# Attention's work lists made cyclic over the batch's end, and PSUM shared as two banks for value sums and two in the ring

## What is computed

```python
x = layernorm(x + attention(x))     # 16 heads of 16 channels, causal
x = layernorm(x + experts(x))       # 8 experts, each token goes to 2; only the first 1024 rows
```

```python
outs.append(_sdpa(q[:, :6], k[:, :6], v[:, :6], 1 / sqrt(16)))          # 6 dot-product heads
outs.append(_hyp_attn(q[:, 6:10], k[:, 6:10], v[:, 6:10], curvature))   # 4 hyperbolic heads
outs.append(_sdpa(qn, kn, v[:, 10:], sqrt(16)))                         # 6 heads of unit q and k
# in _hyp_attn: arg = max(-curv * (q.k - tq * tk), 1 + 1e-7)
#               scores = 1 / (1e-6 + sqrt(1/curv) * arccosh(arg)) + causal mask
```

## Time and profile before

| | us |
|---|---|
| median of 3 runs | 2300.5 (2297.19 to 2304.39) |
| the profiled execution | 2313.54, span on the core 2312.0 |
| TensorE busy | 1806.9 (78%) |
| VectorE busy | 1422.5 (62%) |
| ScalarE busy | 1422.3 (62%) |
| GpSimd busy | 683.8 (30%) |

### The profile page before, as it was taken

The page is one execution under the profiler, slowest core; times in us unless marked ns, Lnnn a source line. Parts: engine busy times, 40 slices in busy tenths (PEclk is TensorE's granted clock), DMA queues, the critical chain, the costliest instruction groups (busy, mean ns, idle before and its releaser), DMA issues. The chain is left out here.

```text
span 2312.0 us, 39981 instructions
## 1 busy us (share of the span) xinstructions
PE 1806.9 (78%) x13330; PEld 965.2 (42%) x13330; DVE 1422.5 (62%) x3280; ACT 1422.3 (62%) x1400; POOL 683.8 (30%) x332
## 2 busy tenths in 40 slices
PE   6888888843887896897797787888789689746994
PEld 3434443421333443343344343444434334325893
DVE  4767676772663776676676777776777667650113
ACT  1333333321887888788788888788788878811110
POOL 0000000001443534444444444543444365510002
PEclk9999999975997998998998999999899899878997
DMA  5222333328026006207306304504502620119972
GB/s 190 85 103 109 110 110 110 110 107 166 1 45 96 11 16 125 66 1 122 83 2 113 92 2 84 121 2 70 126 11 31 137 55 23 42 51 350 345 276 66
DMA packets 88461, 217.50 MB, mean 94 GB/s; under 512 B 14112, under 2 KB 34848, under 8 KB 83936
## 3 DMA queue, kind: packets, MB, share of 16 engines
q1 hardware_dynamic: 79840, 184.74, 30.5%
q0 software_dynamic: 8448, 30.41, 4.2%
HBM read 146.52 MB, written 68.58 MB: 93 GB/s over the span
## 5 line engine op out<-in xcount | busy, mean ns | idle before, releaser
L1067 ACT ACTIVATE a_PT<-a_s 128x1024 f32<-128x1024 f32 (+3 forms) x576 | 461.3, 808 | 206.8 <-PE a_s L889 135.0
L886 PE MATMUL a_s<-a_Q,a_K 96*128 96x512 bf16 (+7 forms) x1152 | 331.3, 350 | 157.0 <-ACT a_PT L1067 108.7
L1245 DVE TENSOR_REDUCE a_mx<-a_w 128x1 f32<-128x512 f32 (+2 forms) x576 | 305.9, 550 | 53.0 <-PE a_w L917 36.8
L1145 POOL TENSOR_TENSOR a_Z<-a_Z,a_R 128x2182 f32<-128x2182 f32 x64 | 290.4, 4537 | 94.0 <-ACT a_R L1079 94.0
L1142 POOL TENSOR_TENSOR a_R<-a_Z 128x2182 f32<-128x2182 f32 x64 | 244.6, 3822 | 217.2 <-DVE a_Z L1237 130.7
L245 PE MATMUL p_ps<-p_xT,p_w 128*128 128x512 f32 x512 | 248.0, 645 | 46.4 <-ACT p_xT L341 25.5
L901 PE MATMUL a_o<-a_PT,a_V 128*32 128x512 f32 (+3 forms) x2304 | 276.0, 554 | 6.4 <-ACT a_PT L1067 6.4
L1237 DVE TENSOR_SCALAR_CACHE_REDUCE a_Z<-a_w 128x512 f32<-128x512 f32 (+7 forms) x384 | 202.0, 530 | 120.2 <-PE a_w L929 85.3
L946 PE MATMUL a_w<-a_ident,a_R 128*128 128x128 f32 (+1 forms) x1152 | 207.4, 306 | 75.2 <-DVE a_PTh L1294 63.9
L1294 DVE COPY a_PTh<-a_w 128x512 f32<-128x512 f32 (+1 forms) x256 | 156.4, 618 | 141.0 <-PE a_w L946 138.8
L886 PEld LDWEIGHTS a_s<-a_Q,a_K 99*128 99x128 bf16 (+1 forms) x1152 | 111.0, 102 | 250.5 <-ACT a_PT L1067 140.6
(11 more groups left out here) (161 smaller groups left out, 2961.9 us busy)
## 6 DMA issues: line engine op xcount, KB each, us to landing
e_w<-in_w SPq DMA_DIRECT2D x23, 2048.0 KB, 8.5
qk_parts<-p_parts SPq DMA_DIRECT2D x32, 768.0 KB, 3.5
a_Q<-qk_parts SPq DMA_DIRECT2D x144, 128.0 KB, 4.7
a_K<-qk_parts SPq DMA_DIRECT2D x144, 128.0 KB, 6.6
v_rows<-p_vt SPq DMA_DIRECT2D x8, 2048.0 KB, 7.7
a_V<-v_rows SPq DMA_DIRECT2D x32, 512.0 KB, 8.1
p_xin<-in_x SPq DMA_DIRECT2D x8, 1024.0 KB, 6.7
a_X<-in_x POOLq DMA_DIRECT2D x8, 1024.0 KB, 11.3
```

The costliest lines, as they stand in the source:

```text
L886: m = pe.matmul(sB[x % 2][:, i, 0:w], Kb[0:r, h, P * j:P * j + P], Qb[0:r, h, t0:t0 + w], start=True, stop=not diag)
L1067: act.activation(PT[:, u % 2, 2 * k:2 * k + 2, 0:w], sB[x % 2][:, :, 0:w], ACT.Exp, scale=scale_of(GROUPS[g][2 * k])).then_inc(prob.sem, 1)
L1145: pool.tensor_tensor(z, z, r, ALU.add).then_inc(z_sum.sem, 1)
L1245: dve.tensor_reduce(mx[:, pc, col:col + 1], wB[x % WB][:, 0:w], AX.X, ALU.max).then_inc(wide_free.sem, 1)
```

## The change

- The eight units start at `LEAD` 12 and are spread over `SPAN` 122 positions (before 6 and 113). Unit 7 is ready at 134 and all of it after `add_root`, and the end of unit 6, wraps into the next pass.
- Both rounds of maxima begin one step later; the second has one step less. `turn_sums` of five tiles move later (tile 2 from 125 to 143, tile 3 from 161 to 178, tile 4 from 165 to 181).
- The ring has two banks, and `a_o` two: one for each half of the tokens, so a half waits for the copy of the half before last.
- `turn_sums` of tiles 0 to 3 of the batch before now come after the first `sums` of the batch. So this first copy goes to a new tile `early`, and a new GpSimd item `unstage` at position 41 copies it into `O`; `turn_sums` of tile 0 waits for that, and the next `early` copy too.

```diff
--- before.py
+++ after.py
@@ -632,7 +632,7 @@
             work[u][VALUES if u < NQ else 0].append(("values", u - 1))
             if (u - 1) % 12 in (3, 11):
                 work[u][VALUES + 1 if u < NQ else 0].append(("sums", 2 * ((u - 1) // 12) + ((u - 1) % 12 == 11)))
-        LEAD, LAST = 6, 113
+        LEAD, SPAN = 12, 122
         wrapped = set()
 
         def put(at, item):
@@ -643,9 +643,9 @@
             work[at // NSLOT][at % NSLOT].append(item)
 
         for n in range(NU):
-            ready = LEAD + LAST * n // (NU - 1)
+            ready = LEAD + SPAN * n // (NU - 1)
             args = [("argument", n, k, pc) for k, seg in enumerate(segments(n)) for pc in range(len(seg[3]))]
-            span = 2 * len(args) if n else LEAD
+            span = 2 * len(args) if n else 8
             for a, item in enumerate(args):
                 put(ready - span + a * span // len(args), item)
             put(ready, ("square", n))
@@ -666,7 +666,7 @@
                 for part in range(2):
                     put(ready + 37 + part, ("hyp_values", HYP_TILES[n - 1 + part]))
 
-        ROUNDS = (((4, 5), 1, 1, 7), ((0, 1, 2, 3), 2, 8, 13))
+        ROUNDS = (((4, 5), 1, 2, 7), ((0, 1, 2, 3), 2, 9, 12))
         MAXIMA = [[(h, i, pc, s0, w) for h in hs for i in range(NT) for pc, (s0, w) in enumerate(pieces(i))]
                   for hs, _, _, _ in ROUNDS]
         for r, (_, _, first_step, steps) in enumerate(ROUNDS):
@@ -686,9 +686,10 @@
             work[11 + 2 * n][1].append(("project", n))
             work[12 + 2 * n][2].append(("statistics", 0, n, n + 1))
 
-        SUMS = {0: 117, 1: 121, 2: 125, 5: 147, 6: 151, 7: 155, 3: 161, 4: 165}
+        SUMS = {0: 117, 1: 121, 2: 143, 5: 148, 6: 152, 7: 156, 3: 178, 4: 181}
         for n, at in SUMS.items():
             put(at, ("turn_sums", n))
+        put(41, ("unstage",))
         work[2][0].append(("shift",))
         work[27][0].append(("variance", 0))
         work[27][3].append(("inverse_root", 0))
@@ -706,7 +707,7 @@
 
         RINGED = ("argument", "maximum", "turn_maxima", "turn_rows", "project", "turn_sums", "turn", "hyp_values")
         ringed = [item for step in work for slot in step for item in slot if item[0] in RINGED]
-        WB = 3
+        WB = 2
         MORE = -len(ringed) % WB
         n_wide = len(ringed) + MORE
         m_item = ringed.index(("turn_maxima", 1))
@@ -770,6 +771,7 @@
         nb = sb("a_nb", [P, 2, 4])
         PTh = sb("a_PTh", [P, NT + 1, 4, P])
         O = sb("a_O", [P, 4, T])
+        early = sb("a_early", [P, HB])
         X = sb("a_X", [P, NT, C])
         Y = sb("a_Y", [P, NT, H, HD])
         rden = sb("a_rden", [P, 2, H])
@@ -779,7 +781,7 @@
         rs = sb("a_rs", [P, 3, NT])
         first = sb("a_first", [P, C])
         sB = [ctx.enter_context(nc.psum_tensor(f"a_s{i}", [P, 2, HB], F32)) for i in range(2)]
-        oB = psum("a_o")
+        oB = [psum(f"a_o{i}") for i in range(2)]
         wB = [psum(f"a_w{i}") for i in range(WB)]
 
 
@@ -796,7 +798,7 @@
         score = ev("a_score", NQ * 2, carried=True)
         prob = ev("a_prob", NQ * 2, carried=True)
         valued = ev("a_valued", NQ, carried=True)
-        o_copied = ev("a_o_copied", 6, carried=True)
+        o_copied, o_moved = ev("a_o_copied", 6, carried=True), ev("a_o_moved", carried=True)
         wide_full, wide_free = ev("a_wide_full", n_wide, carried=True), ev("a_wide_free", n_wide, carried=True)
         m_step = ev("a_m_step", 12)
         z_sq = ev("a_z_sq", NU)
@@ -895,10 +897,10 @@
                 if j == 0:
 
                     n = 2 * g + c
-                    pe.wait_ge(o_copied.sem, o_copied.at(b, n - 1) if n else o_copied.before(b, 5))
+                    pe.wait_ge(o_copied.sem, o_copied.at(b, n - 2) if n >= 2 else o_copied.before(b, 4 + n))
                     pe.wait_ge(v_here[g].sem, v_here[g].at(b))
                 for k in range(4):
-                    m = pe.matmul(oB[VW * k:VW * k + VW, t0 - HB * c:t0 - HB * c + w], V[:, g, j, k, :],
+                    m = pe.matmul(oB[c][VW * k:VW * k + VW, t0 - HB * c:t0 - HB * c + w], V[:, g, j, k, :],
                                   PT[:, u % 2, k, 0:w], start=(j == 0), stop=(j == 4 * c + 3))
                 m.then_inc(valued.sem, 1)
 
@@ -963,6 +965,8 @@
                 bank = wide_bank(b, index["turn_sums", n])
 
                 pe.wait_ge(o_copied.sem, o_copied.at(d, 4 if n < NT // 2 else 5))
+                if n == 0:
+                    pe.wait_ge(o_moved.sem, o_moved.at(d))
                 pe.wait_ge(wide_free.sem, wide_free.at(*ring(b, d, ("hyp_values", n), index)))
                 for g in range(4):
                     m = pe.transpose(bank[:, g * P:(g + 1) * P], O[:, g, n * P:(n + 1) * P], ident[:])
@@ -1150,6 +1154,11 @@
                     pool.wait_ge(h_prob.sem, h_prob.at(d, 4 * n + 2 * part + 1))
                     edge = R[:, n % RB, at:at + 2 * w].rearrange("p (f s) -> p f s", f=2)[:, :, w - GK:w]
                     pool.tensor_tensor(edge, edge, hmasks[:, 1], ALU.mult).then_inc(h_masked.sem, 1)
+                elif kind == "unstage":
+
+                    pool.wait_ge(o_copied.sem, o_copied.at(d, 0))
+                    hold(pool, wide_full.sem, wide_full.at(b, wide["turn_sums", NT // 2 - 1]), pool_passed)
+                    pool.tensor_copy(O[:, 0, 0:HB], early[:]).then_inc(o_moved.sem, 1)
                 elif kind == "shift":
                     pool.wait_ge(x_here.sem, x_here.at(d))
                     pool.tensor_tensor(X[:], X[:], bias[:].unsqueeze(1).to_broadcast([P, NT, C]), ALU.add) \
@@ -1187,6 +1196,7 @@
                     if is_last and u % 4 == 3 and u // 4 < NT:
                         spread_rows(u // 4)
 
+            o_moved.start(pool)
             rows_in(0)
             turn(0, is_first=True)
             with nc.Fori(1, B - 1, engines=[pool.engine], hint_back_edge=True) as b:
@@ -1306,7 +1316,12 @@
             def copy_sums(b, m):
                 g, c = divmod(m, 2)
                 dve.wait_ge(valued.sem, valued.at(b, 12 * g + (3 if c == 0 else 11)))
-                dve.tensor_copy(O[:, g, HB * c:HB * c + HB], oB[:]).then_inc(o_copied.sem, 1)
+                if m == 0:
+
+                    dve.wait_ge(o_moved.sem, o_moved.before(b))
+                    dve.tensor_copy(early[:], oB[0][:]).then_inc(o_copied.sem, 1)
+                else:
+                    dve.tensor_copy(O[:, g, HB * c:HB * c + HB], oB[c][:]).then_inc(o_copied.sem, 1)
 
             def divide_sums(b, d, n, x):
                 sums = wB[x % WB][:].rearrange("p (h w) -> p h w", w=VW)
```

## The result

| | before | after |
|---|---|---|
| time, median (range) of the runs | 2300.5 us (2297.2 to 2304.4) | 2545.9 us (2526.9 to 2564.8) |
| profiled execution (span) | 2313.5 (2312.0) us | 2529.8 (2528.2) us |
| mean granted clock of TensorE | 0.898 | 0.864 |
| mean of passes 1 to 6 | 184.0 us | 210.1 us |

The change made the kernel 245 us slower: the ratio is 1.107, 95% interval 1.096 to 1.118. Its four times lie in two pairs, 2527 and 2530 us and 2562 and 2565 us, so whatever is subtracted from their median of 2546 us is uncertain by some 25 us. The forecast was 2317.5 us with a range up to 2366: the direction was right, the size was not.

The account below looks back on a forecast made before the run. Bound: hand-overs of small tiles between three in-order engines, none alone. Ring 8 + 1 + 1 - 8.5 gains = +1.5 us a pass, times 8 is +12, ends +5: 2317.5 us from 2300.5; range 2262 to 2366.

Parts of the forecast that it names:

- The ring: Two banks for three: in 40 long gaps a pass the third item waits one more drain; 8 us of at most 24.
- Rival C: The ring costs in full, 18 us a pass: slower by much, 2397 us; chance 0.07.
- The sign I gave the waits: TensorE's waits for L1294, L1245, L1237 rise from some 20 to nearly 30 us a pass; staying at 20 favours faster.
- (a): VectorE's collisions with GpSimd at `normalize` and `join_maxima` go: gains of 3.5, 1 and 1.5 us a pass.
- (b): `turn_sums` of tile 2 moves from one to six positions behind `hyp_values`, shedding its wait: gain of 1 us a pass.
- (c): Balance: activations and exponentials move from positions 132 to 143 into 0 to 16, where ScalarE has room: gain 1.5 us.
- (e): Group 3's Q and K load later, from position 132, and may land late: cost 1 us a pass, bounds 0 and 5.
- (d): `row_bias` stands closer behind GpSimd's `square`; half of eight overlap by up to 1.2 us: cost 1 us, bounds 0 and 4.
- (f): `early` copy and GpSimd's `unstage` at position 41: 0 us, at most 1.1 us a pass; nothing new waited for.
- Value banks: Second bank for `a_o`: removes a wait TensorE never had; 0 us, at most a few tenths.
- The ends: Wrapped items after the last pass cost some 7 us, the first pass saves 2: +5 us.
- D: Rival: the load of (e) comes 5 us late, 4 more than taken, in 7 passes: 2345 us; chance 0.11.

Follow-up runs that it names:

- e1: The kernel before with the ring cut from three banks to two, order and single value bank kept: 2479.8 us, ratio 1.075.
- e7: e6 with GpSimd's shift of X moved from position 8 to 21: 2292.7 us, ratio 0.994.
- e2: The kernel after with three ring banks and one bank for value sums, so the new order alone: 2363.1 us, ratio 1.024.
- e6: e2 with the first round of row maxima one step (four positions) earlier: 2317.2 us, ratio 1.004.
- e3: e1 with two banks for value sums and the wait of the kernel after: 2479.2 us, ratio 1.074.
- e8: The kernel before with `variance` to `rows_out` three or four positions later, off `add_root` of units 6 and 7: 2334.0 us, ratio 1.012.

## Why the prediction was wrong in size, step by step

- **The ring, the step that failed.** "I take a third of the upper, 8 us a pass." Measured alone: 21.5, 90% of the upper end of 24. With it in place of 8 the forecast would have been some 2425 us. The mechanism was right (the third item of a gap waits for one more drain, 40 gaps of that kind); the discount was not. It rested on TensorE's slack ahead of the scores in the earlier trace rows, which was one pass's total. A total doesn't say that the slack lies in the gaps with many items, and there it mostly doesn't: they grew by a whole drain in the mean. The sum also had no term for the stalls that the third bank covered (3.9 us a pass at 132 to 143 in e1). The same rows had said that the ring was a gate already. Rival C (18 a pass, 2397 us) had the right ring and, with the costs of the order missing, still fell short.
- **The sign I gave the waits: the right one, read off too few rows.** TensorE's waits for L1294, L1245 and L1237 were to rise from some 20 to nearly 30 us a pass. The 20 were the two largest groups alone. With all rows of these three drains added up, the weight loads wait 32 us in the pass of before, 54 in e1 and 45 in the kernel after: 21 us more in e1, as much as the ring costs there. In the view of L1245 they rose where the next item is of another kind (L929, L975), hardly on L914. ScalarE's wait for scores, 23 to 52 us, I had not named.
- **(a) Collisions taken off: right.** `normalize` is free now. In the kernel after:
```profile
L1381 DVE TENSOR_TENSOR a_rs<-a_rs x16: 149/162/265, 917.3 to 2295.7; 128x8 f32<-128x8 f32 x16
...
L1261 DVE TENSOR_TENSOR a_mx<-a_mx x16: 164/180/193, 596.4 to 2154.7; 128x16 f32<-128x16 f32 x8, 128x32 f32<-128x32 f32 x8
```
against the 3132 and 1930 ns of the earlier trace rows. L1366 and L1251 were busy 48.7 and 31.4 us in before, and their successors are busy 2.7 and 2.9 us. In e7 positions 108 to 119 take 3.3 us less than in before (3.5 taken), 84 to 95 1.2 us less (1.5 taken). The 1 us at 120 to 131 didn't come, as that stretch grew.
- **What (a) missed.** I asked which collisions go and not which arrive. The cast of `cut_maxima` arrived: 6 us a pass, 46 us in e2, in no term of the sum.
- **(b) and (c) Balance: wrong, as far as is shown.** Taken together as a gain of 2.5 us. In e7, 120 to 131 takes 2.8 us more than in before, 132 to 143 2.0 more, and 24 to 35 2.3 more; 12 to 23 takes 4.7 less, but e7 also has the later shift there, which no run tries in the old order. ScalarE is the bound in two of these: in the kernel after it works 17.52 of 18.48 us at 24 to 35 and 15.47 of 16.31 us at 120 to 131. I had compared stretches of 24 positions; in stretches of 12 the peaks show. They and the next point are why e7 gains only 2.2 us a pass of the 6.5 that (a) to (e) add up to; no run separates the two.
- **(d) too small.** Overlaps of up to 1.2 us in half of the eight were taken. `row_bias`, before and then after (count, busy us, mean ns, idle before):
```profile
L1275 DVE TENSOR_TENSOR a_R<-a_R 128x2 f32<-128x2 f32 x64 | 9.8, 154 | 61.6 <-ACT a_R L1088 61.3
```
```profile
L1285 DVE TENSOR_TENSOR a_R<-a_R 128x2 f32<-128x2 f32 x64 | 49.7, 777 | 42.7 <-ACT a_R L1092 42.7
```
That is 40 us more on VectorE, 5 us a pass: 17 of the 64 take over 1 us, the longest 4.4; in e7 they are busy 53.6 us in all. ScalarE's direct wait for it (the bias L1277, now L1287) rose from 7.5 to 23.7 us, 29.9 in e7, so 2 to 3 us a pass for the 1 taken, inside the bounds of 0 and 4. With the casts (L1264 3.6 us in before, L1274 29.1 us in the kernel after) 65 us of collisions came to VectorE for the 75 that went.
- **(e), (f): about right.** TensorE's matmuls wait 26.8 us in six places for the Q and K of `t_parts`, 19 of it in the first pass, as in before (20.5); about 1 us a pass is left. `unstage` takes 0.68 us and nobody waits for it. But I wrote that `mask` and `square` "wait for nothing new". That holds behind `unstage`; behind the shift of X it fails: 3 us a pass (e6 to e7).
- **Value banks: right in the order of before.** e3 equals e1, and in the kernel after TensorE waits for no copy of `a_o`.
- **The ends.** 5 us taken. From the last exponential for scores to the write of the output there are 66.9 us (2232.9 to 2299.8), against 53.3 before (2026.9 to 2080.2): 13.6 us for the 7 taken. The first pass grew by 19.3 us (220.2 against 200.9) where the others grew by 26.1, so it is 6.8 us better than the rest; I took 2. The mask of a late unit stands behind the shift here too:
```profile
2243.80 4.49 POOL L1164 TENSOR_TENSOR a_X<-a_X,a_bias 128x2048 f32<-128x2048 f32 x1 [5.01 <-DMA a_X<-in_x]
...
2248.76 1.97 PE L948 MATMUL a_w<-a_ident,a_R 128*128 128x128 f32 x8 [11.59 <-POOL a_R L1156]
```
- **The sum by measured terms.** Ring +172, cast +46, shift +24.5, the rest of the order -14.5 (e7's ratio of 0.9937, times 2300): together +228 us. The kernel after is at +245, and its ratio of 1.096 to 1.118 means 220 to 270. So the other 17 us lie inside its scatter; whether the parts cost each other anything is open.
- **The range.** It took the ring's upper end into rival C with a chance of 7 in 100 and let D and the ring not add. The costs added, as far as the scatter lets one tell.

## What to carry to other kernels

When a ring between two in-order engines loses a bank, count the stretches with as many items as there were banks or more, and take one drain for each, in full, unless a row shows slack in those very stretches. Here that fits the mean with full drains (0.56 us); with the short ones the price was 0.14 us per long gap for a drain of 0.22. Look also for every long stall of the draining engine that the extra bank now covers. When an order moves, list every instruction of VectorE that comes to lie beside a long one of GpSimd, casts and copies of any size too, and everything that comes to stand behind an operation that waits for a transfer; here 75 us of them went and 65 us arrived at other instructions. Look at each engine's load in the shortest stretches that the trace allows, since balance over long ones hides the peaks.

## What the hardware showed that I had not expected

- A cast with a single SBUF input is held up until a GpSimd instruction ends: 0.21 us at best, 3.30 us in the row, 4.33 at most. Its size, 16x128 elements, didn't help it.
- It holds the other way round too. In e8 VectorE's `add_bias` began at 1278.07 and GpSimd's L1145 at 1278.15; the latter took 6.89 us in place of 4.80, longer by about the 2.21 us that `add_bias` had still to run. Six of its 64 do this, with 6.33 to 6.89 us. The Trainium skill says in the same section that the order of issue decides which of the two is blocked, and these rows agree.
- A stall can cost TensorE twice. In the stretch with the cast the mean granted clock was 0.65, so part of it was spent at the lower of the two levels, and four turned tiles took 1.11 us at 1230.76, behind 4.29 us of idle time, where they took 0.60 us at 1224.53. TensorE's busy time for the same instructions rose from 151.66 to 164.21 us a pass; how much of that is the clock isn't separated.
- A transfer that has to be over by a certain time is not moved at a constant price: `x_mid` took 5.9 us in its old place and 11.1 us a few positions later, where it ran beside SyncE's loads. That these loads are the cause is argued from the overlap in time, not tested.
